# Three lists of steps laid anew in a kernel that overlaps graph convolution, attention and experts

## The chip, the cores and the metric

The kernel runs on one core of one Trainium2 chip. The metric is the device time of one execution in microseconds (us), as the median of three runs. The engines are PE (TensorE, with its weight loads PEld), DVE (VectorE), ACT (ScalarE), POOL (GpSimd) and SP (SyncE, which here only issues DMAs).

## What is computed

The input is `x`, 16 images of 256 channels on 16 x 16 positions. Cut to what matters:

```python
def reference(x, ...):
    x = x + conv(group_norm(x))          # "L0": two attentions over time and channels, three
                                         # Chebyshev products, a 1x3 convolution, relu, a layer norm
    t = tokens(x)                        # 16 x 256 tokens of 256 features
    t = t + linear_attention(ln(t))      # "L1": causal, 16 heads, phi = elu + 1, then Wo and bias
    t = t + ffn(ln(t))                   # 16 routed experts of 64 (4 chosen per token) + shared 512
    return from_tokens(t)
```

All products are to float32 accuracy. Products with the QKV and expert weights are made of three fp32r products of high and low parts (`mm3`, lines 518 to 520); the others are plain float32 matmuls.

## The kernel before

The 16 images go through as 8 pairs (0 to 7). Of each pair there are five chains of steps, and a step is a few instructions on one or several engines:

- conv (room for one pair at a time from pair 2 on): `gn` (group norm statistics), `xg` (normalise, DVE L918), `xT0 xT1` (transposes, PE L1282, copied by ACT L735), `M prod Epre Eexp Erep lr p2` (the two small attentions), `sp0 sp1` (PE L1345, softmax: DVE maxima L980, ACT exponentials L769), `rv0 rv1` (reciprocals), `st0 st1` (transposes and three products with Chebyshev matrices, DVE L996), `Y0 Y1` (PE L1244), `o0 o1` (PE L1362, 24 matmul records each), `tc0 tc1`.
- tail: `xb` (POOL), `z1` (means), `z2` (variances and a Newton root, DVE L1008 to L1025), `z3` (scale and add: DVE L1031 and L1034 for one image, POOL L689 and L692 for the other).
- attn: `tok0 tok1 nrm xl0 xl1` (layer norm and transposes), `k0 .. q1`, `kt kv`, `dent` (denominators), `rd` (SP writes the denominators to HBM and reads them back spread over partitions), then for four groups `S00 V00 S01 V01 S10 V10 S11 V11` (scores, PE L1230; causal mask, DVE L1084; weighted sums in the PSUM bank `num`, PE L1448 and L1259), `at0 at1` (DVE L1090: `num` times the spread denominators), `wo0 wo1` (DVE L1094 adds).
- route: `tk0 tk1` (transposes; statistics DVE L863, root POOL L698), `nrm2` (ACT L797), `xn0 xn1` (PE L1393), `lg` (logits), `r1 r2 r3 r4 cb` (choice of experts).
- ffn, 12 steps `j`: `gu` (24 products for gate and up), `h` (silu on ACT, product on DVE), `w` (weight of the routed expert on DVE, high part on ACT, low part on POOL), `dn` (12 products into `d_ps`).

Beside them there are steps that occur once: `hot0` to `hot23` (two PE matmul records each on constants, L1267, whose result nobody reads), and `high0` to `high13` (ACT L716) with `low0` to `low13` (DVE L858), which split 14 pieces of the weights, each loaded by one DMA, into high and low parts. `gu0` of pair 0 needs 7 pieces split.

One list, PROGRAM, is the order of all steps, and each engine goes through it and issues its own part of every step. It is put together from three tables: OPENING (pairs 0 to 2, written `pair:step`), BODY (repeated for five turns, with `+n` for the next n ffn steps of the pair that is in its experts), CLOSING (pairs 6 and 7). Every engine is in order, so a step that waits holds up everything behind it on its engine. The PSUM bank of a step is its place in the list modulo 4 (`ring`), and a step waits until the bank's user four fills before has been read.

Two waits matter below. SP issues all loads of the start, among them pieces 0 to 3. Before it issues pieces 4 to 13, and therefore before everything it takes from PROGRAM, it waits for the end of `z3` of pair 1, whose room the pieces overwrite:

```python
                if i == EARLY_PIECES:
                    sp.wait_ge(tail_dve.of(1), tail_dve.at(1, "n30"))
                    sp.wait_ge(tail_pool.of(1), tail_pool.at(1, "n31"))
                sp.dma_start(PIECES[i][3], PIECES[i][0]).then_inc(piece_loaded[i], 16)
```

And `at0` waits both for the sums and for the spread denominators, while `V10` on PE waits for `at0`, which frees `num`:

```python
                    dve.wait_ge(pv_done.of(p), pv_done.at(p, f"V{b}1"))
                    dve.wait_ge(dens_spread, 16 * 2 * (p + 1))
```

Of the kernel before, what the change touches and what calls it, by code (L numbers as in the profile page):

```python
# [118 lines left out]
OPENING = """
    0:gn 1:gn 0:xg 0:xT0 1:xg 0:M 0:xT1 0:Y0 2:gn 0:prod 1:xT0 0:high0 0:Epre 1:M 1:xT1 0:Eexp 1:Y0 1:prod 0:hot0 2:xg  # L120
    0:hot1 0:Erep 0:hot2 1:Epre 1:Eexp 0:lr 2:xT0 0:p2 1:Erep 2:M 0:high1 1:lr 0:sp0 0:rv0 0:xb 1:p2 0:sp1 0:st0
    0:hot3 2:xT1 0:hot4 0:hot5 0:rv1 0:Y1 1:sp0 0:st1 0:o0 0:low0 0:o1 0:low1 1:rv0 0:tc0 0:tc1 1:sp1 2:Y0 0:z1 0:hot6
    1:st0 2:prod 1:rv1 0:hot7 1:Y1 0:z2 0:hot8 1:st1 1:o0 2:Epre 2:Eexp 0:z3 0:high2 1:o1 0:tok0 0:tok1 0:hot9 1:tc0
    1:tc1 0:nrm 0:hot10 0:hot11 1:xb 1:z1 0:hot12 0:low2 0:hot13 2:Erep 0:xl0 0:xl1 0:hot14 1:z2 0:k0 2:lr 0:k1 1:z3
    0:v1 0:q0 0:high3 0:v0 0:kt 0:q1 0:high4 2:p2 0:hot15 0:hot16 0:hot17 0:dent 0:high5 0:high6 0:kv 0:hot18 0:rd
    0:low3 0:S00 0:hot19 2:sp0 0:V00 0:low4 0:S01 2:rv0 2:sp1 0:low5 0:at0 0:V01 0:S10 2:st0 2:rv1 0:high7 0:hot20
    0:V10 0:low6 0:S11 0:hot21 0:hot22 0:V11 2:Y1 0:hot23 0:at1 0:wo0 0:low7 0:wo1 0:high8 0:low8 0:tk0 0:tk1 0:nrm2
    0:high9 2:st1 2:o0 0:xn0 0:xn1 1:tok0 0:high10 1:tok1 1:nrm 2:o1 0:high11 0:low9 0:low10 0:lg 0:low11 1:xl0 1:xl1
    +1 0:r1 +1 1:k0 0:r2 1:k1 0:r3 +3 0:high12 0:high13 1:v1 0:silu 0:r4 1:q0 0:cb 2:xb +1 1:v0 1:kt +1 0:low12 1:q1
    +1 0:low13 +3 1:dent 2:tc0 2:tc1 +1 1:kv +2 1:rd +1 1:S00 +3 0:exp +1 1:V00 1:S01 +2 1:at0 +1 1:V01 +1 1:S10 +3  # L130
    2:z1 +1 1:V10 +1 1:S11 +2 1:V11 2:z2 1:at1 +4 2:z3 1:wo0 +2 1:wo1 +4 1:tk0 1:tk1 +4 1:nrm2 +2 1:xn0 1:xn1 +1 1:exp
"""
# [13 lines left out]


# [1436 lines left out]
```

## Time and profile before

| what | us |
|---|---|
| median of 3 runs | 931.02 (929.78 to 932.94) |
| span of the profiled execution | 958.6 |
| PE busy in it | 920.9 |
| DVE / ACT / POOL busy | 630.1 / 434.7 / 229.5 |
| start of `gu0` of pair 0 on PE | 176.9 |

The profile shows one execution, for which the page gives its span alone; that is 27.6 us longer than the median of the runs. The span has three parts: an opening up to the first `gu0`, in which PE is partly idle; from there to about 936 us PE is busy in almost every slice; and a short end. The clock column of the page is the share of TensorE's clock that was granted: 0.85 for most of the time up to about 416 us, and 0.95 after that.

### The profile page before, as it was taken

The page shows a single profiled execution, that of the slowest core. Times are in us where ns is not written, and L with a number is a line of the kernel's source. Part 1 is how long each engine was busy: PE and PEld are TensorE (multiplying, and loading weights), DVE is VectorE, ACT ScalarE, POOL GpSimd, SP SyncE. Part 2 cuts the span into 40 slices and gives each one's busy share as a digit, 9 for nine tenths or more (in the row PEclk, how much of TensorE's full clock was granted, in tenths as well). Part 3 has the DMA queues.
Part 4 walks back from the last instruction along what each step waited for, and adds up shares of the span by engine and source line. Part 5 has one row for each costly group of instructions (what it writes and reads, how often), then busy time and mean ns, then how long its engine had stood idle before and what let it go on. Part 6 is the DMA issues. An engine that isn't in the chain of part 4 may idle for free.

```text
span 958.6 us, 19446 instructions
## 1 busy us (share of the span) xinstructions
PE 920.9 (96%) x7824; PEld 802.4 (84%) x7824; DVE 630.1 (66%) x1637; ACT 434.7 (45%) x837; POOL 229.5 (24%) x198
## 2 busy tenths in 40 slices
PE   4998988999999999999999999999999999999997
PEld 2576756888898889889898889988898888988997
DVE  5546785777597447965588638975588738774532
ACT  2344443652365524645267334655257434832432
POOL 2113300113221124212241124212241124212222
PEclk9887788888888888899999999999999999999998
DMA  6000050031001110021101110021101200021021
GB/s 228 1 1 1 1 189 1 1 92 36 23 13 59 35 34 23 13 71 34 34 24 35 59 34 23 13 71 34 34 24 34 61 13 23 19 76 35 20 83 34
DMA packets 37961, 39.21 MB, mean 41 GB/s; under 512 B 5232, under 2 KB 34416, under 8 KB 37872
## 3 DMA queue, kind: packets, MB, share of 16 engines
q1 hardware_dynamic: 37872, 37.96, 12.6%
q8 instruction: 63, 1.03, 0.5%
q14 instruction: 26, 0.21, 0.1%
HBM read 32.97 MB, written 4.98 MB: 40 GB/s over the span
## 4 chain that ended last, share of the span: by engine, by line
PE 85%; DVE 10%; ACT 2%; issue 2%; DMA 1%; SPq 0%; POOLq 0%; POOL 0%; DVEq 0%; ACTq 0%
PE ring L1362 10%; PE g_ps L518 5%; PE d_ps L518 4%; PE d_ps L520 4%; PE d_ps L519 4%; PE g_ps L520 4%; PE u_ps L520 4%; PE g_ps L519 4%; PE u_ps L519 4%; PE u_ps L518 4%; PE ring L1230 4%; PE ring L1345 3%; PE num L1259 3%; PE ring L518 3%; PE ring L520 3%; PE ring L519 3%
## 5 line engine op out<-in xcount | busy, mean ns | idle before, releaser
L704 POOL TENSOR_TENSOR hl<-hb,hh 128x512 fp32r<-128x512 f32 x96 | 125.9, 1311 | 424.1 <-ACT hh L835 424.0
L835 ACT ACTIVATE hh<-hb 128x512 fp32r<-128x512 f32 x96 | 60.7, 632 | 137.0 <-DVE hb L1202 116.1
L518 PE MATMUL d_ps<-hh,down_h 128*128 128x256 f32 x384 | 116.6, 304 | 3.0 <-POOL hl L704 2.2
L518 PE MATMUL g_ps<-normed_h,gate_h 128*128 128x256 f32 x352 | 110.0, 312 | 0.2
L519 PE MATMUL d_ps<-hl,down_h 128*128 128x256 f32 x384 | 109.2, 284 | 0.0
L520 PE MATMUL d_ps<-hh,down_l 128*128 128x256 f32 x384 | 109.0, 284 | 0.0
L520 PE MATMUL g_ps<-normed_h,gate_l 128*128 128x256 f32 x352 | 100.2, 285 | 0.0
L520 PE MATMUL u_ps<-normed_h,up_l 128*128 128x256 f32 x352 | 100.1, 284 | 0.0
L519 PE MATMUL u_ps<-normed_l,up_h 128*128 128x256 f32 x352 | 100.0, 284 | 0.0
L519 PE MATMUL g_ps<-normed_l,gate_h 128*128 128x256 f32 x352 | 100.0, 284 | 0.0
L518 PE MATMUL u_ps<-normed_h,up_h 128*128 128x256 f32 x352 | 99.9, 284 | 0.0
L1197 DVE TENSOR_TENSOR hb<-sl,u_ps 128x512 f32<-128x512 f32 x88 | 60.1, 683 | 52.6 <-PE u_ps L520 38.0
L1084 DVE TENSOR_TENSOR shared<-ring,constants 128x512 f32<-128x512 f32 x128 | 79.4, 683 | 18.3 <-PE ring L1230 18.3
L518 PEld LDWEIGHTS d_ps<-hh,down_h 128*128 128x128 f32 x384 | 73.7, 192 | 8.3 <-issue 4.6
L832 ACT ACTIVATE sl<-g_ps 128x512 f32<-128x512 f32 x88 | 52.5, 597 | 59.2 <-PE g_ps L520 58.7
L518 PEld LDWEIGHTS g_ps<-normed_h,gate_h 128*128 128x128 f32 x352 | 67.4, 191 | 11.9 <-issue 6.5
L519 PEld LDWEIGHTS d_ps<-hl,down_h 128*128 128x128 f32 x384 | 73.7, 192 | 1.0 <-issue 0.3
L520 PEld LDWEIGHTS d_ps<-hh,down_l 128*128 128x128 f32 x384 | 73.8, 192 | 0.0
L519 PEld LDWEIGHTS g_ps<-normed_l,gate_h 128*128 128x128 f32 x352 | 67.8, 192 | 3.6 <-issue 3.2
L519 PEld LDWEIGHTS u_ps<-normed_l,up_h 128*128 128x128 f32 x352 | 67.6, 192 | 0.0
L518 PEld LDWEIGHTS u_ps<-normed_h,up_h 128*128 128x128 f32 x352 | 67.6, 192 | 0.0
L520 PEld LDWEIGHTS u_ps<-normed_h,up_l 128*128 128x128 f32 x352 | 67.6, 192 | 0.0
(402 smaller groups left out, 2166.2 us busy)
## 6 DMA issues: line engine op xcount, KB each, us to landing
weights_over_hidden<-weights_by_expert SPq DMA_DIRECT2D x128, 128.0 KB, 3.0
shared<-denominators_by_head SPq DMA_DIRECT2D x16, 256.0 KB
out_x<-kept SPq DMA_DIRECT2D x16, 256.0 KB, 2.2
...
raw_weights<-in_gateT SPq DMA_DIRECT2D x4, 384.0 KB, 6.7
raw_weights<-in_upT SPq DMA_DIRECT2D x4, 384.0 KB, 5.5
raw_weights<-in_down SPq DMA_DIRECT2D x4, 384.0 KB, 8.5
...
```

Of the source, the lines that this page charges most:

```text
L518: eng.matmul(ps, wh, xh, start=start, stop=False, **how)
L519: eng.matmul(ps, wh, xl, start=False, stop=False, **how)
L520: return eng.matmul(ps, wl, xh, start=False, stop=stop, **how)
L704: pool.tensor_tensor(hl[:, j % 2, :], hb, hh[:, j % 2, :].bitcast(F32), ALU.subtract).then_inc(*ffn_pool.mark(p, f"lo{j}"))
L832: act.activation(sl, gate_up(p, j)[0][:, :], ACT.Silu).then_inc(*ffn_act.mark(p, f"si{j}"))
L835: act.activation(hh[:, j % 2, :], hb, ACT.Copy).then_inc(*ffn_act.mark(p, f"hi{j}"))
L1084: dve.tensor_tensor(p_s[:, j, :].rearrange("p (h l) -> p h l", h=4), tile(p, n)[:, :].rearrange("p (h l) -> p h l", h=4), const_at("causal ...
L1197: dve.tensor_tensor(hb, sl, gate_up(p, j)[1][:, :], ALU.mult).then_inc(*ffn_dve.mark(p, f"h{j}"))
L1230: last = pe.matmul(tile(p, n)[:, 2 * c * P:(2 * c + 2) * P], k_f[rows, c, cols], q_eo[rows, :, c, cols], start=True, stop=True, tile_posit ...
L1259: last = pe.matmul(num[rows, c * L + lc * P:c * L + lc * P + P], v_s[:, b, lc, 4 * c + j, 16 * odd:16 * odd + 32], p_s[:, j, (2 * c + odd) ...
L1345: last = pe.matmul(t[:, kc * N:(kc + 1) * N], vs_s[:, jc, kc * P:(kc + 1) * P], g.th[:, b, jc, :], start=(jc == 0), stop=(jc == 1))
L1362: last = pe.matmul(t[:, c * N:(c + 1) * N], g.y_s[b][:, m, c, k], g.a_s[:, k, m, :], start=(k == 0 and m == 0 and c == 0), stop=(k == 2 an ...
```

## The change

The three tables are written anew. Every step occurs as often as before, within each chain the steps stand in one common order for all pairs, and the instructions, buffers, waits and constant products of a step are the same. What changes is where steps stand against those of other chains and pairs. The core of the diff (the rest of the tables is of the same kind):

```diff
 OPENING = """
-    0:gn 1:gn 0:xg 0:xT0 1:xg 0:M 0:xT1 0:Y0 2:gn 0:prod 1:xT0 0:high0 0:Epre 1:M 1:xT1 0:Eexp 1:Y0 1:prod 0:hot0 2:xg
...
+    0:high0 0:gn 0:xg 0:high1 0:xT0 1:gn 0:M 0:xT1 0:hot0 0:Y0 1:xg 2:gn 0:prod 0:hot1 0:low0 1:xT0 2:xg 1:M
+    1:xT1 2:xT0 0:Epre 0:hot2 1:Y0 0:hot3 0:Eexp 2:M 1:prod 2:xT1 0:hot4 0:Erep 1:Epre 2:Y0 0:hot5 0:high2
...
 BODY = """
-    +1 tok0 tok1 lg +1 gn +1 nrm +3 xg r1 +1 xl0 xl1 +1 xT0 r2 +2 M k0 xT1 k1 +2 Y0 r3 silu +1 prod r4 v1 Epre cb Eexp
...
+    +1 tok0 tok1 lg +1 gn +1 nrm +1 r1 +1 xg +3 xl0 xl1 xT0 M r2 +1 k0 xT1 k1 +1 r3 +1 silu +1 Y0 +1 prod r4
...
```

In CLOSING, `6:lg` now stands between `7:tok0` and `7:tok1`, and `7:exp` before the last experts of pair 6 in place of the middle of those of pair 7.

What this does to the engines' own orders is shown at three places.

**Place 1, the opening, DVE.** Before, from `z3` of pair 1 (its row sums lie in `hb`, its squares in `raw_weights`) over `q0`, `q1`, `p2` of pair 2, `dent` and `kv`:

```order
L1031 TENSOR_TENSOR kept<-kept,hb 128x2x256
L1034 TENSOR_TENSOR kept<-kept,raw_weights 128x2x256
L1050 TENSOR_SCALAR shared<-shared 128x512
L1052 SCALAR_TENSOR_TENSOR shared<-ring,shared 128x512
L1063 TENSOR_TENSOR shared<-shared 128x512
L1050 TENSOR_SCALAR shared<-shared 128x512
L1052 SCALAR_TENSOR_TENSOR shared<-ring,shared 128x512
L1063 TENSOR_TENSOR shared<-shared 128x512
L970 TENSOR_TENSOR first<-ring,bs_s 128x512 x2
L1070 TENSOR_SCALAR one_over_denominator<-ring 128x128
L1072 RECIPROCAL one_over_denominator<-one_over_denominator 128x128
L1065 TENSOR_TENSOR shared<-ring,constants 128x512
```

Now (line numbers are 2 higher), from `q1` over the maxima of `sp0` of pair 2, `dent`, `kv` and `z3` of pair 1 to the masks of `S00`, the reciprocal and maxima of pair 2, one split and the masks of `S01`:

```order
L1052 TENSOR_SCALAR shared<-shared 128x512
L1054 SCALAR_TENSOR_TENSOR shared<-ring,shared 128x512
L1065 TENSOR_TENSOR shared<-shared 128x512
L982 TENSOR_REDUCE conv_small<-ring 128x2
L1072 TENSOR_SCALAR one_over_denominator<-ring 128x128
L1074 RECIPROCAL one_over_denominator<-one_over_denominator 128x128
L1067 TENSOR_TENSOR shared<-ring,constants 128x512
L1033 TENSOR_TENSOR kept<-kept,hb 128x2x256
L1036 TENSOR_TENSOR kept<-kept,raw_weights 128x2x256
L1086 TENSOR_TENSOR shared<-ring,constants 128x512 x4
L986 RECIPROCAL conv_small<-conv_small 128x2
L982 TENSOR_REDUCE conv_small<-ring 128x2
```

`z3` of pair 1 has moved from ahead of `q0` to directly ahead of the masks of `S00`.

**Place 2, every turn of the body, DVE.** Before, from `wo1` over `h9`, `w9`, the statistics of `tk0 tk1`, `h10`, `w10` and the shift of `nrm2` to `z3` of the next pair:

```order
L1094 SCALAR_TENSOR_TENSOR kept<-ring,small_parameters,kept 128x512
L1197 TENSOR_TENSOR hb<-sl,u_ps 128x512
L1202 TENSOR_TENSOR hb<-hb,weights_over_hidden 128x512
L863 BN_STATS tst<-ring 128x6 x4
L514 MEMSET carrier 1x1
L870 BN_AGGR tmv<-tst 128x2 x4
L872 TENSOR_SCALAR tve<-tmv 128x4
L1197 TENSOR_TENSOR hb<-sl,u_ps 128x512
L1202 TENSOR_TENSOR hb<-hb,weights_over_hidden 128x512
L876 SCALAR_TENSOR_TENSOR shift<-tmv,trs 128x4
L1031 TENSOR_TENSOR kept<-kept,row_sums 128x2x256
L1034 TENSOR_TENSOR kept<-kept,filters 128x2x256
```

Now:

```order
L1096 SCALAR_TENSOR_TENSOR kept<-ring,small_parameters,kept 128x512
L1199 TENSOR_TENSOR hb<-sl,u_ps 128x512
L1204 TENSOR_TENSOR hb<-hb,weights_over_hidden 128x512
L1033 TENSOR_TENSOR kept<-kept,row_sums 128x2x256
L1036 TENSOR_TENSOR kept<-kept,filters 128x2x256
L865 BN_STATS tst<-ring 128x6 x4
L516 MEMSET carrier 1x1
L872 BN_AGGR tmv<-tst 128x2 x4
L874 TENSOR_SCALAR tve<-tmv 128x4
L1199 TENSOR_TENSOR hb<-sl,u_ps 128x512
L1204 TENSOR_TENSOR hb<-hb,weights_over_hidden 128x512
L878 SCALAR_TENSOR_TENSOR shift<-tmv,trs 128x4
```

The two instructions of `z3` have moved from behind the shift to ahead of the statistics; POOL's two of the same step move with them.

**Place 3, the start, ACT.** Before, the end of `Y0` of pair 0, then the first split (`high0`, L716):

```order
L747 ACTIVATE kept<-ring 128x2x2x32
L744 ACTIVATE shared<-ring 128x12x32
L747 ACTIVATE kept<-ring 128x2x2x32
L752 ACTIVATE shared<-shared 16x32
L735 ACTIVATE raw_weights<-ring 128x512
L716 ACTIVATE wqkv_h<-raw_weights 128x768
L756 ACTIVATE shared<-shared 16x32
L735 ACTIVATE raw_weights<-ring 128x512
```

Now, from the first instruction that computes:

```order
L713 ACTIVATE router<-small_parameters 128x2x16
L718 ACTIVATE wqkv_h<-raw_weights 128x768 x2
L737 ACTIVATE shared<-ring 128x512 x2
L746 ACTIVATE shared<-ring 128x12x32
L749 ACTIVATE kept<-ring 128x2x2x32
L746 ACTIVATE shared<-ring 128x12x32
```

The first two splits have moved ahead of the first transposed copy of pair 0.

## Rows read from the trace of the kernel before

**Rows 1.** The page: busy time, share of the span and instructions of each engine.

```profile
PE 920.9 (96%) x7824; PEld 802.4 (84%) x7824; DVE 630.1 (66%) x1637; ACT 434.7 (45%) x837; POOL 229.5 (24%) x198
```

**Rows 2.** Windows: length, busy time of PE, PEld, DVE, ACT, POOL, granted clock, DMA.

```profile
0.00:13.00 13.00, 1.22 (x5) 1.06 (x5) 6.23 (x36) 1.51 (x2) 4.67 (x16) 1.00 0.88 277
13.00:177.00 164.00, 147.36 (x1001) 107.85 (x1002) 103.65 (x248) 68.13 (x168) 27.22 (x23) 0.84 0.12 40
...
263.40:379.20 115.80, 115.80 (x975) 101.52 (x973) 77.10 (x203) 53.30 (x104) 28.27 (x23) 0.85 0.11 34
...
598.30:706.60 108.30, 108.15 (x974) 96.12 (x973) 76.19 (x203) 53.20 (x104) 28.32 (x23) 0.95 0.12 36
```

**Rows 3.** Windows again, the same columns, three stretches of the opening.

```profile
13.00:38.50 25.50, 22.07 (x152) 14.06 (x152) 15.04 (x59) 8.96 (x28) 4.98 (x4) 1.00 0.20 73
...
76.00:79.00 3.00, 3.00 (x36) 2.44 (x36) 1.03 (x2) 1.31 (x5) 0.00 (x0) 0.51 0.00 0
...
107.00:113.00 6.00, 5.33 (x18) 3.22 (x18) 5.46 (x18) 1.73 (x4) 2.32 (x2) 0.50 0.00 0
```

**Rows 4.** Timeline of PE, opening: start, length, operation, idle before and its releaser.

```profile
16.13 1.12 PE L1282 MATMUL ring<-constants,shared 128*128 128x128 f32 x4
18.09 2.09 PE L1244 MATMUL ring<-theta_s,shared 32*128 32x128 f32 x32 [0.84 <-ACT shared L735]
...
23.10 0.42 PE L1311 MATMUL ring<-shared,ve_h 16*64 16x32 f32 x2
...
50.89 0.66 PE L1282 MATMUL ring<-constants,first 128*128 128x128 f32 x4
...
57.44 12.21 PE L1362 MATMUL ring<-shared 128*128 128x256 f32 x48
```

**Rows 5.** The start: timeline of ACT, of SP, and the page's DMA row.

```profile
23.70 0.83 ACT L716 ACTIVATE wqkv_h<-raw_weights 128x768 fp32r<-128x768 f32 x1
...
9.24 0.94 SPq L586 DMA_DIRECT2D raw_weights<-in_wqkvT  x2
...
raw_weights<-in_wqkvT SPq DMA_DIRECT2D x2, 384.0 KB, 6.9
```

**Rows 6.** Timeline of DVE, from `z3` of pair 1 to `at0` of pair 0.

```profile
119.73 0.67 DVE L1031 TENSOR_TENSOR kept<-kept,hb 128x512 f32<-128x512 f32 x1
120.42 0.69 DVE L1034 TENSOR_TENSOR kept<-kept,raw_weights 128x512 f32<-128x512 f32 x1
...
129.19 2.48 DVE L1084 TENSOR_TENSOR shared<-ring,constants 128x512 f32<-128x512 f32 x4 [0.58 <-PE ring L1230]
...
140.67 0.69 DVE L1090 TENSOR_TENSOR shared<-num,shared 128x512 f32<-128x512 f32 x1 [0.65 <-DMA shared<-denominators_by_head]
```

**Rows 7.** Timeline of SP's queue, and its own waits (us in total, times, longest).

```profile
121.14 0.33 SPq L586 DMA_DIRECT2D raw_weights<-in_gateT  x1
...
127.41 0.70 SPq L609 DMA_DIRECT2D denominators_by_head<-one_over_denominator  x1
135.11 1.26 SPq L612 DMA_DIRECT2D shared<-denominators_by_head  x2
...
SPq L612 <- DMA denominators_by_head<-one_over_denominator: 22.6, 8, 7.0
```

**Rows 8.** Timeline of PE: the last part of `V01`, and `V10`, of pair 0.

```profile
138.88 1.19 PE L1259 MATMUL num<-shared,v_s 128*32 128x128 f32 x32
...
144.30 1.16 PE L1259 MATMUL num<-shared,v_s 128*32 128x128 f32 x32 [0.68 <-DVE shared L1084]
```

**Rows 9.** Timelines of DVE, POOL, ACT and PE in one turn of the body.

```profile
587.84 1.42 DVE L863 BATCH_NORM_STATS2 tst<-ring 128x6 f32<-128x256 f32 x4
...
590.06 1.02 POOL L698 TENSOR_TENSOR trs<-tve,minus_half 128x4 f32<-128x4 f32 x1
...
593.04 1.91 ACT L797 ACTIVATE shared<-ring,shift,trs 128x256 f32<-128x256 f32 x4
...
595.10 1.08 PE L1393 MATMUL ring<-constants,shared 128*128 128x128 f32 x8 [0.26 <-ACT shared L797]
```

More of the change, by code:

```diff
@@ L119 @@
 OPENING = """
-    0:gn 1:gn 0:xg 0:xT0 1:xg 0:M 0:xT1 0:Y0 2:gn 0:prod 1:xT0 0:high0 0:Epre 1:M 1:xT1 0:Eexp 1:Y0 1:prod 0:hot0 2:xg
[L121 to L129, printed above, removed]
@@ L130 @@
-    +1 0:low13 +3 1:dent 2:tc0 2:tc1 +1 1:kv +2 1:rd +1 1:S00 +3 0:exp +1 1:V00 1:S01 +2 1:at0 +1 1:V01 +1 1:S10 +3
-    2:z1 +1 1:V10 +1 1:S11 +2 1:V11 2:z2 1:at1 +4 2:z3 1:wo0 +2 1:wo1 +4 1:tk0 1:tk1 +4 1:nrm2 +2 1:xn0 1:xn1 +1 1:exp
+    0:high0 0:gn 0:xg 0:high1 0:xT0 1:gn 0:M 0:xT1 0:hot0 0:Y0 1:xg 2:gn 0:prod 0:hot1 0:low0 1:xT0 2:xg 1:M
+    1:xT1 2:xT0 0:Epre 0:hot2 1:Y0 0:hot3 0:Eexp 2:M 1:prod 2:xT1 0:hot4 0:Erep 1:Epre 2:Y0 0:hot5 0:high2
+    0:hot6 1:Eexp 0:lr 1:Erep 1:lr 0:p2 1:p2 0:sp0 0:rv0 1:sp0 1:rv0 2:prod 0:sp1 0:st0 1:sp1 2:Epre 0:rv1
@@ new lines @@
+    0:hot7 0:hot8 0:hot9 0:Y1 2:Eexp 0:hot10 0:st1 0:low1 0:high3 1:st0 0:o0 0:o1 0:xb 0:tc0 0:tc1 1:rv1 1:Y1
+    0:z1 2:Erep 0:z2 0:z3 1:st1 1:o0 0:tok0 0:tok1 0:nrm 0:low2 1:o1 0:xl0 0:xl1 1:tc0 1:tc1 0:k0 0:k1 0:v1
+    1:xb 0:q0 2:lr 1:z1 0:v0 0:hot11 0:kt 2:p2 1:z2 0:q1 2:sp0 0:dent 0:hot12 0:kv 0:rd 0:hot13 0:hot14 1:z3
+    0:S00 2:rv0 2:sp1 0:high4 0:low3 0:V00 0:S01 0:hot15 0:hot16 2:st0 0:at0 0:V01 0:high5 0:high6 0:hot17
+    0:S10 0:high7 0:hot18 0:V10 2:rv1 0:low4 0:high8 0:S11 0:low5 0:hot19 0:hot20 0:hot21 0:hot22 0:V11 2:Y1
@@ new lines @@
+    0:at1 0:high9 0:high10 0:low6 0:low7 0:low8 0:hot23 0:wo0 0:wo1 0:tk0 0:tk1 0:nrm2 2:st1 2:o0 0:xn0 0:xn1
+    1:tok0 0:high11 0:high12 1:tok1 0:low9 0:high13 1:nrm 2:o1 0:low10 +1 0:low11 +1 0:lg 0:r1 1:xl0 +1 1:xl1
+    0:r2 0:r3 +3 1:k0 1:k1 +1 0:silu 1:v1 0:r4 +2 2:xb 0:cb 1:q0 1:v0 1:kt 1:q1 2:tc0 2:tc1 +2 1:dent 0:low12
+    +1 1:kv +3 1:rd 1:S00 0:exp +1 0:low13 1:V00 +3 1:S01 1:at0 +1 1:V01 +3 1:S10 +3 1:V10 +3 2:z1 +3 1:S11
+    +2 1:V11 1:at1 +2 2:z2 1:wo0 1:wo1 2:z3 +1 1:tk0 +3 1:tk1 +5 1:nrm2 +1 1:xn0 1:xn1 1:exp +1
@@ L132 @@
 """
 BODY = """
-    +1 tok0 tok1 lg +1 gn +1 nrm +3 xg r1 +1 xl0 xl1 +1 xT0 r2 +2 M k0 xT1 k1 +2 Y0 r3 silu +1 prod r4 v1 Epre cb Eexp
-    q0 v0 kt q1 Erep +2 lr dent kv +3 rd S00 +2 V00 S01 +1 p2 at0 +1 V01 S10 +2 sp0 +1 rv0 +1 sp1 st0 +1 rv1 Y1 V10
-    st1 +1 o0 +3 S11 +2 V11 o1 at1 xb +2 tc0 tc1 z1 wo0 +4 z2 wo1 +4 tk0 tk1 +4 nrm2 +1 z3 +1 xn0 xn1 +1 exp
+    +1 tok0 tok1 lg +1 gn +1 nrm +1 r1 +1 xg +3 xl0 xl1 xT0 M r2 +1 k0 xT1 k1 +1 r3 +1 silu +1 Y0 +1 prod r4
+    v1 cb Epre Eexp q0 v0 kt q1 +2 Erep dent kv +1 rd lr +2 S00 +2 p2 +1 V00 +1 S01 at0 +2 V01 S10 +2 sp0 rv0
@@ L138 @@
+    sp1 +1 st0 +1 V10 +2 S11 +1 rv1 +1 Y1 xb V11 +1 at1 st1 o0 +1 o1 tc0 tc1 +1 z1 wo0 +4 z2 +1 wo1 +3 z3 tk0
+    tk1 +4 nrm2 +2 xn0 xn1 +1 exp
 """
 CLOSING = """
-    +1 7:tok0 7:tok1 +2 7:nrm 6:lg +1 7:xl0 +2 7:xl1 +1 6:r1 6:r2 6:r3 +1 7:k0 6:silu 6:r4 6:cb 7:k1 +2 7:v1 7:q0 +2
-    7:v0 7:kt 7:q1 +3 7:dent 7:kv 7:rd +3 7:S00 +2 7:V00 7:S01 +2 7:at0 +2 7:V01 7:S10 +4 7:V10 7:S11 +4 7:V11 +1
-    7:at1 +1 7:wo0 +1 7:wo1 +4 7:tk0 7:tk1 +3 7:nrm2 +2 7:xn0 7:xn1 +3 7:lg +1 7:r1 +3 7:r2 7:r3 +2 7:silu +1 7:r4
@@ L144 @@
-    7:cb +27 7:exp +22
+    +1 7:tok0 6:lg 7:tok1 +2 7:nrm +1 6:r1 +3 6:r2 +1 6:r3 7:xl0 6:silu 7:xl1 +1 6:r4 +2 6:cb +1 7:k0 7:k1
+    7:v1 7:q0 7:v0 +1 7:kt +1 7:q1 +1 7:dent 7:kv +2 7:rd +1 7:S00 +3 7:V00 +1 7:S01 +2 7:at0 7:V01 +2 7:S10
+    +1 7:V10 +1 7:S11 +4 7:V11 +3 7:at1 7:wo0 7:wo1 +2 7:tk0 7:tk1 +2 7:nrm2 +3 7:xn0 7:xn1 +3 7:lg +2 7:r1
+    +1 7:exp +3 7:r2 7:r3 +1 7:silu +1 7:r4 7:cb +50
 """
```

## Prediction

> **What bounds the kernel now.** I read the page first: PE is busy for 920.9 us, 96% of the span [rows 1], so what an order of steps can change is PE's 37.7 us of idleness, its clock, and new waits. The windows say where these lie. Up to 13 us PE did 1.2 us of work; from 13 to 177 us, when the experts of pair 0 begin, it was busy for 147.4 of 164 us, so 16.6 us idle; a body turn is full, 115.8 of 115.8 us at a granted clock of 0.85 and 108.15 of 108.3 us at 0.95 [rows 2]. A turn has hardly anything to give, and everything to lose from a new wait. The opening has 16.6 us of waits and a slow clock besides: four transposes took 1.12 us at 16 us and 0.66 us at 51 us [rows 4], which puts the first stretch at 1.2 GHz (the window shows 1.00 there only because the profile holds no clock record before 38 us), and 76 to 79 and 107 to 113 us were granted 0.5 again [rows 3].
>
> **How the profile stands to the runs.** The profiled span is 958.6 us, the median 931.02. Part of that is the clock: a turn at 0.85 takes 7.5 us more than one at 0.95 [rows 2]. The terms below are waits for DVE and DMA, which do not shorten with TensorE's clock; I work them out against the 958.6 us and add them unscaled to 931.0.
>
> **Term 1, the spread denominators of pair 0: +9 us.** This is what I rest on. Before, DVE ended `z3` of pair 1 at 121.11 (120.42 + 0.69) [rows 6]. SP had been waiting for that: it issued the ten remaining pieces from 121.14, the write of the denominators at 127.41, and their spreading reads only at 135.11, because the write landed late [rows 7]. The longest of the eight waits for that write was 7.0 us and all eight were 22.6 us, so the others took 15.6 / 7 = 2.2 us each [rows 7]: this one stood behind ten pieces of 384 KB each. `at0` started at 140.67, after 0.65 us of waiting for the spread data [rows 6]. From the end of that `z3` to `at0` is thus a chain of 140.67 - 121.11 = 19.6 us, all of it SP and DMA, and nothing in it is changed.
>
> What lies beside it is. Before, the masks of `S00` began at 129.19 [rows 6] and `V01`, the other thing that `at0` needs, ended at 138.88 + 1.19 = 140.07 [rows 8], 10.9 us later. The two chains arrived together, because `z3` came 8.1 us ahead of the masks. Now `z3` of pair 1 stands directly ahead of the masks of `S00` on DVE (place 1), behind `q1` and `kv` of pair 0, so both chains start at one point: the denominators need 19.6 us, the sums about 10. (Of the 10.9 us, two splits of 0.95 us leave the stretch on DVE, and 1.9 us of Chebyshev products of pair 2 come in ahead of `at0`.) `at0` is late by 19.6 - 10.5 = 9 us. Whatever the opening did up to there, this difference stays. Queued behind `at0` on DVE are the masks of `S10`, a split and the masks of `S11`; on PE, `V10` waits for `at0`, and everything behind it in the list, up to the first `gu0`, waits on PE. What is ahead of `V10` (`V01`, `S10`, two `hot`) covers no more than before: it is already inside the 10.9 us or follows it by 4 us, as `V10` did (144.30 [rows 8]). Bounds: 7 us if `S00` is itself held by `qo1` or the second image's maxima, 10.5 if the sums need no more than 9.
>
> **The DMA rule beside it.** The Trainium skill (DMA: Bandwidth & Descriptors, Queues, rings and completion order) says that completion is not first-in first-out per issuing engine: a later, smaller DMA can be complete while an earlier one is not. By that the 64 KB write might take the 2.2 us of the other turns rather than the 7.0 us of the row, and term 1 would be about 4 us instead of 9. The row is of this very situation and decides.
>
> **Term 2, the clock after that wait: +1 us.** PE would stand still for some 9 us. In the trace its clock was at 0.50 from 107 to 113 us, where it had waited more than once in the microseconds ahead [rows 3]. One such stretch costs half of its 5.3 us of PE work, 2.7 us, and some of the 18 us of transposes, scores and `hot` behind `V10` wait for DVE anyway. Bounds 0 and 3; I take 1. The Trainium skill (TensorE: Matmul & The Clock Gate, HAM oscillation) says that an idle gap of this kind brings the clock down and that a slow stretch costs half its length; by the rule alone I would write 3.
>
> **Term 3, the rest of the opening: 0 us, between -8 and +4.** All 24 `hot` stand ahead of the first `gu0` as before, and of real work only `lg` of pair 0 and `xl0 xl1` of pair 1 (3.1 us) now come after it, so only waits and clock count. At the start DVE saves: `xg` of pair 0 no longer stands behind the statistics of pair 1, some 3.5 us. ACT takes that away (place 3): the two splits now precede the first copy. Their pieces were issued from 9.24 and need 6.9 us [rows 5], so the second is there at about 16.8 and the copy starts 0.8 us later, near 17.7; `Y0` starts near 19 instead of 18.09 [rows 4]. Then `Epre` of pair 0 (23.10 before [rows 4]) stands behind `xg` and `xT0` of pair 2; `xg` (1.7 us of DVE) waits for a root on POOL that itself follows `Y0`'s copies. I put `Epre` at about 29, and `o0` (57.44 before [rows 4]) at about 66. But by then PE has also done `Y0` and both `sp` of pairs 2 and 1, `st0` of pair 1 and five more `hot`, some 8 us: even. The upside is the clock. At 13 to 38.5 us 22.1 us of PE work ran at the lower level and 107 to 113 another 5.3 us [rows 3], and seven `hot` instead of three now stand ahead of `p2`. If these lift the clock ten microseconds earlier, PE does that work in half the time, but copies and reciprocals between the products don't shorten. Hence -8 as one end; +4 is what `Epre`, 6 us late, could leave.
>
> **Term 4, the five turns of the body: +4 us.** (a) `z3` of the next pair now stands ahead of the statistics of `tk0 tk1` on DVE (place 2). Its two instructions take 0.67 + 0.69 us (their equals in [rows 6]), and POOL's two of the same step now precede the root there. The chain statistics 587.84, root 590.06, normalising 593.04, `xn0` 595.10 already ends last: PE waited 0.26 us for it [rows 9]. Of the 1.4 us some is absorbed, since the shift waited behind `w10` before; I take +0.5 us a turn, with 0 and 1.4 as ends. (b) At the turn's start `r1` (2.1 us of DVE) has moved ahead of `out1` and `xg`, and `M` follows `xT0` at once where an expert step stood between: +0.3 us a turn. Sum 0.8 x 5 = 4 us; bounds 0 and 8. Nothing in a full turn can pay back more than the 0.15 us that PE is idle in it [rows 2].
>
> **Closing: 0 us**, +-1: `lg` of pair 6 gives `tok1` more cover, and the table change of `7:exp` now falls where ACT already has the exponential's table.
>
> **Sum.** 9 + 1 + 0 + 4 = +14, so 931 + 14 = **945 us**.
>
> **Rivals.**
> (A) The opening gains at its front, and the wait of term 1 stays: -8 + 9 + 1 + 4 = +6, 937 us. For it: `hot` steps reach further forward. Against: the copies that pace `Y0` are on ACT and don't shorten. Chance 0.2.
> (B) Faster: the clock. With the clock at its upper level from about 20 us and never back to 0.50, PE saves up to half of (22.1 + 5.3 + three short stretches of 3 us, of which one is shown) = 36 us, 18 us; less the 14 of the other terms, this gives -4, 927 us. It decides against me from 14 us recovered, that is with more than three quarters of all slow work undone. [...] Against: term 1 makes a new idle stretch. The Trainium skill (TensorE: Matmul & The Clock Gate, Part 1) has it so, that sustained activity lifts the clock; by that rule alone B would be likelier than I make it. Chance 0.12, and with it all other ways to end faster.
> (C) The write does not queue behind the pieces, or the sums are themselves late by other waits, so that term 1 is 0 to 4 and the body keeps its 108.3 us: +0 to +4, 933 us. Chance 0.13; two fifths of it are within 0.3%.
> Forecast as summed, +9 to +20: chance 0.55.
>
> **How the numbers follow.** A measurement of this kernel tells about 0.3%, 3 us, from no change. Slower than that: the forecast, A, and three fifths of C, 0.83; the same 0.05; faster 0.12. The range runs from 930, which leaves out B's better half and a little more, to 952 (9 + 3 + 2 + 7); the forecast's own range is 940 to 951.
>
> **What would show it.** In the profile after: the `at0` of pair 0 some 19 to 20 us behind the end of `z3` of pair 1, with about 9 us of waiting for the spread DMA on DVE; PE idle for 8 to 10 us ahead of `V10`, and the granted clock at 0.50 around it; `gu0` of pair 0 some 7 to 11 us later than 176.9; turns of the body 0.5 to 1 us longer at equal granted clock, with the wait ahead of `xn0` near 0.8 us. I would be wrong if `S00` began well behind `z3`, if the clock was up from 20 us on, or if a turn lost several us at a place that I took to be covered.

## The result, and the profile after

| what | before | after |
|---|---|---|
| median, us | 931.63 (929.78 to 932.94, 4 runs) | 971.86 (971.12 to 974.49, 4 runs) |
| ratio | 1 | 1.0455, interval 1.0421 to 1.049 |
| span of the profiled execution | 958.6; 929.3 in the second profile (below) | 969.3 |
| PE busy in it | 920.9 | 900.5 |

The change costs 40.2 us. I had forecast slower, by 14. The page of the changed kernel, the row that answers to [rows 1]:

```profile
PE 900.5 (93%) x7824; PEld 792.4 (82%) x7824; DVE 651.6 (67%) x1637; ACT 427.7 (44%) x831; POOL 232.3 (24%) x198
```

Windows of the same kernel, for [rows 2] and [rows 3]: the opening, the stretch around `V10` of pair 0, a body turn from `lg` to `lg`, and the microseconds on both sides of one `xn0` of the body.

```profile
13.00:177.00 164.00, 136.61 (x982) 104.38 (x983) 104.83 (x246) 68.41 (x167) 27.85 (x23) 0.89 0.12 40
...
138.00:150.00 12.00, 2.00 (x34) 1.51 (x32) 4.01 (x7) 1.64 (x3) 0.00 (x0) 0.64 0.20 70
...
599.50:711.70 112.20, 108.17 (x976) 96.21 (x974) 79.62 (x203) 53.29 (x104) 28.61 (x23) 1.00 0.11 35
...
476.00:482.70 6.70, 4.41 (x36) 4.04 (x34) 3.64 (x8) 2.62 (x6) 4.59 (x4) 1.00 0.01 4
482.70:486.10 3.40, 3.31 (x16) 3.34 (x17) 2.01 (x4) 2.35 (x4) 0.00 (x0) 0.50 0.02 5
```

A turn of the body is now 112.2 us long, and PE is idle in 4.0 of them; in five turns that is the large part of the loss. The waits of PE, summed over the execution (us, times, longest), show where:

```profile
PE ring L1395 <- ACT shared L799: 12.3, 6, 2.4
PE num L1261 <- DVE shared L1086: 10.9, 3, 10.0
...
PE g_ps L520 <- DVE hb L1199: 4.8, 6, 1.0
```

The first row is the wait ahead of `xn0`, the second the one ahead of `V10` in the opening, the third the one ahead of `gu9`.

### The profile page after: what moved, and what is told of

It reads as the page before. It is cut to its first block, busy times and chain, and to the rows that moved or that the text cites. A ratio compares the mean times of both kernels' runs of the same rounds, so it can differ in the third digit from the quotient of the medians.

```text
span 969.3 us, 19440 instructions
## 1 busy us (share of the span) xinstructions
PE 900.5 (93%) x7824; PEld 792.4 (82%) x7824; DVE 651.6 (67%) x1637; ACT 427.7 (44%) x831; POOL 232.3 (24%) x198
## 3 DMA queue, kind: packets, MB, share of 16 engines
q1 hardware_dynamic: 37872, 37.96, 12.6%
## 4 chain that ended last, share of the span: by engine, by line
PE 71%; DVE 13%; issue 6%; POOL 3%; ACT 3%; DMA 2%; SPq 1%; POOLq 0%; DVEq 0%
PE ring L1364 8%; PE d_ps L520 4%; PE g_ps L520 4%; PE ring L1232 4%; PE d_ps L522 4%; PE d_ps L521 4%; PE num L1261 3%; PE g_ps L522 3%; PE u_ps L522 3%; PE g_ps L521 3%; PE u_ps L521 3%; PE u_ps L520 3%; PE ring L520 3%; PE ring L1347 3%; PE ring L522 3%
## 5 line engine op out<-in xcount | busy, mean ns | idle before, releaser
L520 PE MATMUL g_ps<-normed_h,gate_h 128*128 128x256 f32 x352 | 108.0, 307 | 4.9 <-DVE hb L1199 4.8
L522 PE MATMUL d_ps<-hh,down_l 128*128 128x256 f32 x384 | 108.3, 282 | 0.0
L522 PEld LDWEIGHTS g_ps<-normed_h,gate_l 128*128 128x128 f32 x352 | 66.3, 188 | 0.0
```

Source lines behind the costliest of these rows:

```text
L520: eng.matmul(ps, wh, xh, start=start, stop=False, **how)
L522: return eng.matmul(ps, wl, xh, start=False, stop=stop, **how)
```

## The experiments

**A second profile of the kernel before, and the halves of the change.** Four kernels: before unchanged, and before with one of the three changed tables.

> The kernel before, unchanged, profiled a second time, because its first profiled span (958.6 us at a granted clock of 0.90) was 27 us above its own median. Theory (the first profile was taken at a lowered clock, and the runs are not): span near 930 us, granted clock 0.97 or more outside the opening, a body turn of about 105 us (108.5 us at 0.95 and 115.8 us at 0.85, carried on to 1.00) and PE waits in a turn no longer hidden. Rival (the profile itself costs the 27 us): span again near 958 us.

> Only OPENING is the new one; BODY and CLOSING are those of before. My prediction's terms 1 to 3 are all in it. Theory P (as predicted, wait of at0 in the opening): +8 to +12 us over before, with 10 us of PE idleness ahead of V10 of pair 0. Theory Q (the wait is partly paid back by the earlier front of the opening, since gu0 of pair 0 started at 176.0 in the changed kernel and 176.9 in the first profile of before): 0 to +6 us.

> Only BODY is the new one. Theory Q (the body is where the size was missed: a turn went from about 105 us at full clock to 112.2 us): +30 to +37 us over before, the turns at 112 us with PE waits ahead of gu9, tk0 and xn0 (1.0, 0.8 and 2.5 us). Theory P (as predicted): +4 us, at most +8, turns of 106 us, and the missing 25 us are elsewhere.

> Only CLOSING is the new one. Both theories: within 2 us of before. If it is +5 us or more, the missing time is partly here, and the sum of the three lists must come to +40 us.

| kernel | median, us | ratio to before, interval | loss at 930.2 |
|---|---|---|---|
| before_again | 931.15 (one run) | | |
| opening_alone | 943.51 | 1.0148 (1.0109 to 1.0187) | 13.3 |
| body_alone | 957.17 | 1.0276 (1.0219 to 1.0333) | 27.0 |
| closing_alone | 930.21 | 1.0009 (0.9988 to 1.0030) | 0 |

The parts add up to 40.3 us. The whole change cost 40.2 us by the medians and 42 us by the ratio, so within the noise nothing is lost or gained by putting them together. Against what was expected, opening_alone lies 1.3 us above its range and body_alone 3 us below its own. The second profile of before has a granted clock of 1.00 throughout the body; the turn that answers to those of [rows 2] is this window:

```profile
463.60:571.30 107.70, 107.08 (x976) 95.52 (x974) 76.15 (x203) 53.36 (x104) 28.33 (x23) 1.00 0.13 36
```

So at full clock a turn before takes 107.7 us with 0.6 us of PE idle (not the 105 us that I had carried on from the lower clocks), and the changed turn is to be set against this one, not against the 115.8 and 108.3 us of the first profile: +4.5 us a turn.

**The opening: the write behind the pieces.** The changed opening, with only SP's order edited: first the write and the spreading reads of the denominators of pair 0, then the ten late pieces.

```diff
-            for i in range(len(PIECES)):
-                if i == EARLY_PIECES:
...
                 if name == "rd":
                     spread_denominators(p)
+                    if p == 0:
+                        late_pieces()
```

> The changed OPENING alone (943.5 us), in which SP issues the write and the spreading reads of the denominators of pair 0 first and the ten late pieces after them. Theory 1, the denominators' write is late because SP holds it behind `z3` of pair 1 and because it stands behind ten pieces of 384 KB: the reciprocal ends at 122.4, the write then lands some 3 us later and the reads are issued near 126 instead of 138.5; `at0` no longer waits 9.6 us for DMA. The pieces are issued 2 us later, and the first split of them stands between the masks of `S00` and `S01`, which can cost 2 to 3 us. Sum 943.5 - 9.6 + 2.5 = 936.4 us (933 to 939). Theory 2, the write takes its 7 us wherever it stands: the reads come at about 131, `at0` near 137, and the ten pieces are late by 8 us, for which the splits wait: 940 us or above.

Measured: 933.52 us, ratio 1.0041 (1.0023 to 1.0058), 10.0 us less than opening_alone. The changed kernel first, in the timelines of SP, DVE and PE (start, length, idle before in brackets):

```profile
126.21 0.33 SPq L588 DMA_DIRECT2D raw_weights<-in_gateT  x1
...
132.82 0.66 SPq L611 DMA_DIRECT2D denominators_by_head<-one_over_denominator  x1
139.83 1.25 SPq L614 DMA_DIRECT2D shared<-denominators_by_head  x2
...
125.50 0.69 DVE L1036 TENSOR_TENSOR kept<-kept,raw_weights 128x512 f32<-128x512 f32 x1
...
145.06 0.69 DVE L1092 TENSOR_TENSOR shared<-num,shared 128x512 f32<-128x512 f32 x1 [8.69 <-DMA shared<-denominators_by_head]
...
148.29 1.94 PE L1261 MATMUL num<-shared,v_s 128*32 128x128 f32 x32 [10.00 <-DVE shared L1086]
```

And opening_reads_first, the same engines:

```profile
123.96 0.66 SPq L613 DMA_DIRECT2D denominators_by_head<-one_over_denominator  x1
126.47 1.26 SPq L616 DMA_DIRECT2D shared<-denominators_by_head  x2
127.85 0.39 SPq L590 DMA_DIRECT2D raw_weights<-in_gateT  x1
...
136.26 0.68 DVE L1096 TENSOR_TENSOR shared<-num,shared 128x512 f32<-128x512 f32 x1
...
140.32 1.08 PE L1265 MATMUL num<-shared,v_s 128*32 128x128 f32 x32 [2.06 <-DVE shared L1090]
```

The reader is to see three things. The write alone has its reads issued 2.51 us behind it, where behind ten pieces it took 7.01. In all, the reads go out 13.4 us earlier: 4.5 us of this are the write's shorter way, and 8.9 us are SP's order, since the write no longer waits for `z3` of pair 1 and for the issue of ten pieces. `at0` starts at 136.26 with no wait, 8.8 us earlier: the sums were ready by then, as the prediction had it. And `V10` takes 1.08 instead of 1.94 us: after the 10 us of idleness it had run at the lower clock level. Theory 1 holds, and the pieces' later issue cost nothing that can be seen: DVE does not wait for one of them ahead of its splits.

**The body, `z3`.** The changed body with `z3` put back behind the statistics; with `wo1` put back too; and, in a third kernel, with only POOL's two instructions of `z3` issued behind the root.

```diff
-z2 +1 wo1 +3 z3 tk0 tk1 +4 nrm2 +2 xn0 xn1
+z2 +1 wo1 +3 tk0 tk1 +4 nrm2 +1 z3 +1 xn0 xn1
```

> The changed BODY alone (957.2 us), with `z3` put back behind the statistics of `tk0 tk1` (the turn ends `z2 +1 wo1 +3 tk0 tk1 +4 nrm2 +1 z3 +1 xn0 xn1`). Theory 1, `z3` delays the root: in the changed turns PE waits 2.4 us for the normalised tokens ahead of `xn0`, before only 0.3, and the chain to it is longer by both instructions of `z3` on DVE (1.4 us), by POOL's two of the same step ahead of the root and by a shift that takes 1.24 instead of 0.16 us. With `z3` behind, that wait is again about 0.4 us, each turn is 2.1 us shorter and the time is 957.2 - 5 x 2.1 = 946.7 us (944 to 950). Theory 2, the chain is late from its start, because `wo1` and the `kept` sums now stand one expert step later: the wait ahead of `xn0` stays above 1.5 us and the time at 954 or above.

> As body_z3_back, and `wo1` too is back ahead of `gu9` (`z2 wo1 +4` in place of `z2 +1 wo1 +3`); from `z1` on the turn is that of before. Theory 1: in the changed turns `gu9` waits 0.76 us on PE for `h8` on DVE, because nothing stands between `gu8` and it; with `wo1` in between the wait goes, and the time falls by another 5 x 0.8 = 4 us, to about 942.5 us (940 to 946). What is left over the 930.2 of before, about 12 us, is then the front half of the turn (`r1` ahead of `xg`, `M` directly behind `xT0`, `Y0`, `p2`), where the waits I can see sum to only some 0.6 us a turn, 3 us in all. Theory 2: the waits in the turn are not independent, and when the late half is restored the front half absorbs what it lost: 933 to 936 us. Theory 3, `wo1`'s place costs nothing: the time is that of body_z3_back within 1 us.

> The changed BODY alone (957.2 us), in which only POOL does its two instructions of `z3` later, behind the root of `tk1`; DVE keeps its two where the change put them, ahead of the statistics. Theory 1a, POOL is what costs: the root started 1.3 us after its variances were there because POOL was still at `z3`, and the shift took 1.24 instead of 0.16 us beside POOL; with the root ahead the first part goes, 1.3 us a turn, and the time is about 950.7 us (948 to 953). Theory 1b, DVE's 1.4 us is what costs: the statistics start as late as before, and nothing changes, 956 to 958 us. Theory 1c: the pair of POOL only moves onto the shift and slows DVE's small instructions there as much as it delayed the root: 954 to 957 us with the wait ahead of `xn0` near 2 us still.

| kernel | median, us | ratio to before, interval |
|---|---|---|
| body_z3_back | 940.52 | 1.0111 (1.0088 to 1.0134) |
| body_z3_wo1_back | 940.60 | 1.0104 (1.0078 to 1.0130) |
| body_z3_pool_later | 944.17 | 1.0158 (1.0137 to 1.0179) |

`z3` alone is worth 16.6 us by the medians (15.3 by the ratios), more than the 10.5 I had expected, and POOL's half of it 13.0 (11.0 by the ratios) where I had expected 6.5. In the changed kernel (timelines of DVE, POOL, ACT and PE, one turn):

```profile
587.98 1.41 DVE L865 BATCH_NORM_STATS2 tst<-ring 128x6 f32<-128x256 f32 x4
...
593.05 1.24 DVE L878 SCALAR_TENSOR_TENSOR shift<-tmv,trs 128x4 f32<-128x4 f32 x1 [0.91 <-POOL trs L700]
...
589.17 1.05 POOL L691 TENSOR_TENSOR kept<-kept,row_sums 128x512 f32<-128x512 f32 x1
590.30 1.29 POOL L694 TENSOR_TENSOR kept<-kept,filters 128x512 f32<-128x512 f32 x1
591.54 1.47 POOL L700 TENSOR_TENSOR trs<-tve,minus_half 128x4 f32<-128x4 f32 x1
592.99 1.28 POOL L706 TENSOR_TENSOR hl<-hb,hh 128x512 fp32r<-128x512 f32 x1
...
594.32 1.93 ACT L799 ACTIVATE shared<-ring,shift,trs 128x256 f32<-128x256 f32 x4 [1.51 <-DVE shift L878]
...
596.39 1.06 PE L1395 MATMUL ring<-constants,shared 128*128 128x128 f32 x8 [2.39 <-ACT shared L799]
```

The same chain in the second profile of before, for [rows 9]:

```profile
560.87 1.42 DVE L863 BATCH_NORM_STATS2 tst<-ring 128x6 f32<-128x256 f32 x4
...
563.10 1.02 POOL L698 TENSOR_TENSOR trs<-tve,minus_half 128x4 f32<-128x4 f32 x1
...
565.47 0.16 DVE L876 SCALAR_TENSOR_TENSOR shift<-tmv,trs 128x4 f32<-128x4 f32 x1
...
566.12 1.92 ACT L797 ACTIVATE shared<-ring,shift,trs 128x256 f32<-128x256 f32 x4
...
568.18 1.06 PE L1393 MATMUL ring<-constants,shared 128*128 128x128 f32 x8 [0.28 <-ACT shared L797]
```

This is the one turn of five in which `xn0` waits at all. The waits of PE in the first profile of before, and the same row in the second, are:

```profile
PE ring L1393 <- ACT shared L797: 0.3, 1, 0.3
```

The row in [rows 9] was thus that of one turn; in the other four the chain was covered. In the turn shown it was 7.31 us from the statistics to `xn0` and is 8.41, and the statistics themselves start behind 1.3 us of `z3` on DVE. The root starts 3.56 us after the statistics instead of 2.23, because POOL is at `z3`, and takes 1.47 instead of 1.02 us; and the shift, an instruction on 128 x 4 numbers, takes 1.24 instead of 0.16 us, because POOL begins `w10` in the same moment, having been held up. In body_z3_pool_later the root starts as soon as its input is there, but the shift is then beside POOL's `z3`, and still takes 1.02 us:

```profile
572.42 1.02 POOL L701 TENSOR_TENSOR trs<-tve,minus_half 128x4 f32<-128x4 f32 x1 [0.88 <-DVE tve L877]
573.41 1.27 POOL L692 TENSOR_TENSOR kept<-kept,row_sums 128x512 f32<-128x512 f32 x1
...
573.68 1.02 DVE L881 SCALAR_TENSOR_TENSOR shift<-tmv,trs 128x4 f32<-128x4 f32 x1
...
576.82 1.06 PE L1398 MATMUL ring<-constants,shared 128*128 128x128 f32 x8 [0.71 <-ACT shared L802]
```

From the start of `gu11` to the start of `xn0` a turn of the changed body takes 5.50 us, in body_z3_pool_later 3.71, and in the second profile of before 2.90 in four turns and 3.27 in the one shown; 2.5 us in five turns make 12.6 of the 16.6 us. Most of the rest is the clock: the last window above shows 3.4 us at 0.50 right behind the 2.3 us of idleness ahead of an `xn0`, half of which is lost, and such a stretch stands in two of the five turns of the changed body and in none of body_z3_back. That is 1.7 us for each stretch, 3.4 in all, and with the 12.6 it makes 16.0, between the 15.3 and the 16.6 measured.

`wo1` is a miss: the wait ahead of `gu9` went (it was 3.8 us in five turns), and the one ahead of `tk0` grew by 5.2 us. Waits of PE in body_z3_wo1_back, to be set against 3.1 us for the same row in body_z3_back:

```profile
PE ring L1387 <- DVE kept L1095: 8.3, 6, 1.5
```

DVE, which adds `wo1`, was late either way; theory 3 holds as long as DVE is late. Whether the place of `wo1` would cost something with DVE in time, no run shows. What makes DVE late is the next test.

**The body, `w7`.** One step moved back in body_z3_wo1_back, and the same step moved forward in the kernel before.

```diff
-o0 +1 o1 tc0 tc1 +1 z1
+o0 +2 o1 tc0 tc1 z1
```

> body_z3_wo1_back (940.6 us, turns of 109.4 us against 107.5 before) with one more place restored: `w7` ahead of `o1` instead of directly ahead of `z1` (`+2 o1 tc0 tc1 z1` in place of `+1 o1 tc0 tc1 +1 z1`). Theory 1, two engines get in each other's way: in the changed turns POOL's 1.29 us for the low part of `w7` falls on the two scalings of `z1` on DVE, which then take 2.40 instead of 1.28 us; the second `wo1` sum on DVE is 1.1 us later, and PE waits 1.66 instead of 0.52 us ahead of `tk0`. With `w7` done earlier the two scalings take 1.28 us again and the wait is back at 0.5: 940.6 - 5 x 1.1 = 935.1 us (933.5 to 937). Theory 2, `tk0` is late because `o0`, `o1` and `tc` stand later in the turn, whatever POOL does: the wait stays above 1.4 us and the time at 939 to 942. The Trainium skill (SBUF - State Buffer, Who interferes with whom) says that an instruction of VectorE with two inputs in SBUF and one of GpSimd that reads SBUF exclude each other; by that it is theory 1.

> The kernel before with one edit: `w7` directly ahead of `z1` in the body (`xb +1 tc0 tc1 +1 z1` in place of `xb +2 tc0 tc1 z1`). Theory 1: no instruction is added and DVE does nothing for `w7`, yet the two scalings of `z1` on DVE now meet POOL's low part of `w7` and take 2.40 instead of 1.28 us, and the wait ahead of `tk0` grows from 0.52 to about 1.6 us: 930.2 + 5.5 = 935.7 us (933.5 to 937). Theory 2: in this turn `tc` ends at another time than in the changed one, so the two do not meet, or the wait is elsewhere: 929 to 932 us.

Measured: body_w7_earlier 935.63 us, ratio 1.0061 (1.0039 to 1.0082), 4.0 to 5.0 us less than body_z3_wo1_back by ratio and by median; before_w7_late 935.47 us, ratio 1.0060 (1.0039 to 1.0082), 5.7 us more than before. Both theories 1. The wait of PE ahead of `tk0`, first in before_w7_late and then in the second profile of before:

```profile
PE ring L1386 <- DVE kept L1094: 8.2, 6, 1.5
...
PE ring L1386 <- DVE kept L1094: 2.6, 6, 0.9
```

In before_w7_late (timelines of DVE and POOL) the two scalings of `z1`, and a few microseconds earlier the masks of `S11`:

```profile
535.48 2.48 DVE L1084 TENSOR_TENSOR shared<-ring,constants 128x512 f32<-128x512 f32 x4 [0.41 <-PE ring L1230]
...
551.01 2.41 DVE L1004 SCALAR_TENSOR_TENSOR kept<-row_sums,kept 128x512 f32<-128x512 f32 x2
...
536.23 1.15 POOL L676 TENSOR_TENSOR filters<-x_s,small_parameters 128x512 f32<-128x512 f32 x1
...
550.97 1.29 POOL L704 TENSOR_TENSOR hl<-hb,hh 128x512 fp32r<-128x512 f32 x1 [4.46 <-ACT hh L835]
```

In the second profile of before, POOL is idle at this place and the scalings take half:

```profile
549.75 1.28 DVE L1004 SCALAR_TENSOR_TENSOR kept<-row_sums,kept 128x512 f32<-128x512 f32 x2
```

The scalings, with both inputs in SBUF, grow by 1.13 us beside 1.29 us of POOL; the masks, whose input is the PSUM bank `ring`, take their usual 2.48 us beside POOL's work.

**The body, `M`, `xg` and `r1`.** Three kernels: `dn0` again between `xT0` and `M`; `r1` again behind `xg`, with `M` left directly behind `xT0` (both on top of body_w7_earlier); and `r1` ahead of `xg` in the kernel before.

```diff
-xT0 M r2 +1 k0
+xT0 r2 +1 M k0
...
-nrm +1 r1 +1 xg +3 xl0
+nrm +2 xg r1 +3 xl0
```

> As body_w7_earlier, and `M` no longer follows `xT0` at once: `dn0` stands between them again (`xT0 r2 +1 M` in place of `xT0 M r2 +1`). Theory 1: `M` waits for ACT's copy of `xT0`, and PE's step from `xT0` to `M` took 1.27 instead of 0.36 us; with 1.5 us of other work between them 0.9 us a turn go, another 4.5 us: 930.6 us (929 to 932.5), and nothing of the body's 27 us is left. Theory 2: the copy is late anyway and the wait goes to `k0` or `xT1`: less than 2 us of gain, 933 us or above.

> As body_w7_earlier (935.6 us), `M` directly behind `xT0` as the change has it, but `r1` behind `xg` again (`nrm +2 xg r1 +3` in place of `nrm +1 r1 +1 xg +3`). Theory 1: the wait ahead of `M` is for `xg`, and `xg` is late because `r1` stands ahead of it on DVE (1.7 us) and because it then meets POOL's low part of `w0` and takes 2.7 instead of 1.75 us. With `r1` behind, `xg` takes 1.75 us and ends before `xT0` is reached, and the 0.9 us a turn go as they did with `dn0` in between: 931.1 us (929.5 to 932.5). Theory 2, what `M` waits for is ACT, as I expected of body_w7_M: `xg`'s place changes nothing, 935 us or above.

> The kernel before, with `r1` ahead of `out1` and `xg` in the body (`nrm +1 r1 +2 xg` in place of `nrm +3 xg r1`). Theory 1: `xg` meets POOL's low part of `w0` here too and takes 2.7 us, ending some 3 us later than before; the last transposes of `xT0` wait 0.3 us for it, `M` is covered by `dn0`: 5 x 0.3 = 1.5 us, 931.3 us (930 to 933). Theory 2: the delay of `xg` goes on into `Y0` and the products behind it: 934 us or above.

| kernel | median, us | ratio to before, interval |
|---|---|---|
| body_w7_M | 931.07 | 1.0014 (0.9998 to 1.0030) |
| body_xg_first | 930.24 | 1.0023 (1.0006 to 1.0040) |
| before_r1_ahead | 931.78 | 1.0025 (1.0005 to 1.0045) |

The number expected of body_w7_M came, its mechanism did not: `M` starts before ACT's copy of `xT0` ends (611.07 against 611.33 in the turn below), and reads `xg`. The changed kernel (DVE, POOL, PE), then body_xg_first:

```profile
608.21 2.71 DVE L920 TENSOR_SCALAR first<-x_s,conv_small 128x256 f32<-128x256 f32 x4
...
608.57 1.28 POOL L706 TENSOR_TENSOR hl<-hb,hh 128x512 fp32r<-128x512 f32 x1 [2.19 <-ACT hh L837]
...
609.79 0.90 PE L1284 MATMUL ring<-constants,first 128*128 128x128 f32 x4
611.07 1.07 PE L1296 MATMUL ring<-first,small_parameters 128*32 128x256 f32 x16 [0.37 <-DVE first L920]
```

```profile
471.98 1.76 DVE L919 TENSOR_SCALAR first<-x_s,conv_small 128x256 f32<-128x256 f32 x4
...
473.69 1.29 POOL L705 TENSOR_TENSOR hl<-hb,hh 128x512 fp32r<-128x512 f32 x1 [2.19 <-ACT hh L836]
...
474.93 0.60 PE L1283 MATMUL ring<-constants,first 128*128 128x128 f32 x4
475.46 1.07 PE L1295 MATMUL ring<-first,small_parameters 128*32 128x256 f32 x16
```

With `r1` ahead, `xg` meets POOL's part of `w0` and takes 2.71 instead of 1.76 us; `xT0` ends late, and `M` starts 1.28 us after `xT0` does instead of 0.53. Either cure takes all or most of it back: cover for `M` (4.5 us by the medians), or `xg` out of POOL's way (3.5 us by the ratios, which leave body_xg_first 2.1 us above before, 0.6 to 3.7). `r1`'s place alone, with the cover of `dn0`, costs 2.3 us (0.5 to 4.2) in before.

**All cures at once**, on the whole changed kernel:

> The changed kernel with the five edits together: the reads of the denominators ahead of the late pieces, and in the body `z3` behind the statistics, `wo1` ahead of `gu9`, `w7` ahead of `o1`, `dn0` between `xT0` and `M`. All else in the three lists is as changed. If the causes found are all and add up: 930.2 + 3.4 (the rest of the opening, as in opening_reads_first) + 0 + 0 = 933.6 us (931.5 to 935.5). If the two halves of the change disturb each other, or much of the loss lay in the order that is left: 938 us or above.

Measured: 935.76 us, ratio 1.0066 (1.0045 to 1.0087), 6.1 us over before. Some 34 of the 40 us are gone with five small edits. The result is 2 us above the sum I had expected. That sum put nothing for the body; by the ratios it would be 3.8 us for the opening and the 1.3 us that body_w7_M is above before, 5.1 us, and the 6.1 measured (4.2 to 8.1) cannot be told from it. No version beats the kernel before.

## Why the prediction was wrong

**Direction right, size wrong: 971.9 us against 945, outside the range to 952.** The step that failed is the fourth term, "the five turns of the body: +4 us"; it measured +27. What it lacked is POOL: its two instructions of `z3` ahead of the root were named and put at nothing (11 to 13 us), and that they and other instructions of POOL can hold up one of DVE has no price in it.

**The signs.** Those of term 1 came, as the next paragraph shows. `gu0` of pair 0 started at 176.0 us, not 7 to 11 us behind the 176.9 of the first profile. That was no gain: the 176.9 belongs to the lower clock, and the second profile of before has `gu0` at 165.6, so that it was 10.4 us later. The turns grew by 4.5 us and the wait ahead of `xn0` reached 2.4, where I had put 0.5 to 1 and 0.8; "if a turn lost several us" was the sign of being wrong that came true.

**Term 1 and 2, the denominators and the clock behind them: +10 predicted, 10.0 measured** (opening_alone less opening_reads_first). From the end of `z3` of pair 1 to `at0` it is 18.9 us (forecast 19.6), DVE waits 8.69, PE 10.0 ahead of `V10`, and in the window from 138 to 150 us the granted clock is 0.64 on the mean, 0.50 (the 1.2 GHz level) behind the wait. The write took 7.0 us behind the pieces, as in [rows 7], and 2.5 alone. The agreement to the microsecond is partly luck, since the two ratios leave some 4 us of room on either side. The DMA rule that I weighed against the row was the wrong half of its section: the Trainium skill (DMA: Bandwidth & Descriptors, Queues, rings and completion order) also says that the increment of the semaphore lands only after every earlier write of the same DMA engine; with that the page and the rows agree.

**Term 3, the rest of the opening: 0 predicted, +3.4 measured** (opening_reads_first over before, interval 2.1 to 5.4), near its upper bound of 4. In the profiles the first `gu0` is 2.2 us late (167.8 against 165.6), although the 3.1 us of `lg` and `xl0 xl1` now come behind it, so the loss lies ahead of it. PE at the front of the opening in the changed kernel, for [rows 4]:

```profile
15.43 1.12 PE L1284 MATMUL ring<-constants,shared 128*128 128x128 f32 x4
...
18.85 2.09 PE L1246 MATMUL ring<-theta_s,shared 32*128 32x128 f32 x32 [1.45 <-ACT shared L737]
...
28.25 0.42 PE L1313 MATMUL ring<-shared,ve_h 16*64 16x32 f32 x2
...
32.69 0.66 PE L1284 MATMUL ring<-constants,first 128*128 128x128 f32 x4
```

`Y0` started at 18.85 and `Epre` at 28.25, as put (19 and 29). The clock did rise at the front, four transposes taking 0.66 us at 32.69, but at 36.34 the 32 products of a `Y0` took 2.09 us again, and the rise did not pay for the rest: rivals A and B fall, and C with them, since the write did queue behind the pieces.

**Term 4, (a), `z3` ahead of the statistics: 0.5 us a turn predicted, with 1.4 as the upper end; 3.3 measured** (16.6 / 5). I named POOL's two instructions in one clause and put no number on them, though the root is the next link of the chain, and they alone are 13.0 of the 16.6 us (body_alone less body_z3_pool_later; 11.0 of 15.3 by the ratios). I also took the wait of [rows 9] for that of every turn, where it stood in one of five. Then I let the shift's wait behind `w10` absorb part of the delay; the shift grew by 1.1 us in its place. And behind the 2.4 us wait the clock came down in two of the five turns, which I had allowed for in the opening only.

**Term 4, (b), `r1` ahead of `xg`, `M` directly behind `xT0`: 0.3 us a turn predicted, about 0.9 measured** (4.5 / 5, body_w7_earlier less body_w7_M). The steps were named rightly; the size lacked POOL again.

**Missed altogether: `w7` directly ahead of `z1`, 1.0 us a turn** (5.0 / 5, with `wo1` back in its place; 5.7 / 5 in before). The prediction has no word on it, and the order of no single engine shows it: DVE does nothing for `w7`.

By the medians these are 16.6 + 5.0 + 4.5 = 26.1 of 27.0 us, and body_w7_M, which undoes all of them, cannot be told from before (ratio 0.9998 to 1.0030). Closing: 0 predicted, 0 measured.

**What the terms have in common.** The three unpriced costs all come from POOL, in two ways. With `w7` and `xg` an instruction of DVE takes about a microsecond longer because POOL works beside it. With `z3` the larger part is POOL's own order: when its two instructions went behind the root, the way from `gu11` to `xn0` fell from 5.50 to 3.71 us, although the shift still took 1.02 us beside POOL. That leaves 0.7 us a turn for the slow shift and for `z3` on DVE together. The first profile of before showed two instructions holding each other up, and I did not look for it: POOL's low part of `w10` took 1.80 us beside DVE's `z3`, in place of 1.28. The upper end of term 4 was a sum of DVE's own durations. The Trainium skill (SBUF — State Buffer, Who interferes with whom) has the rule: VectorE with two inputs in SBUF, or in a two-port mode such as `tensor_scalar` can take, excludes a GpSimd instruction that reads SBUF, and the second blocks until the first has finished. The traces agree: +1.13 us beside 1.29 (scalings of `z1`), +1.08 beside 1.28 (shift), +0.95 beside 1.28 (`xg`), nothing for the masks with their input in PSUM. Only the scalings' collision was made and unmade by itself; for the shift and `xg` the rows show the overlap, and the edits that remove it move other things too.

**The profile.** The first profile of before was of an execution at a granted clock of 0.85 to 0.95. There PE is the slower part of every race, so DVE's and POOL's delays find more cover: PE's waits ahead of `tk0` sum to 1.6 us there and to 2.6 at full clock, and "0.15 us idle in a turn" [rows 2] was 0.6. The wait ahead of `xn0` was 0.26 us there and 0.28 at full clock, so this did not hide the chain. Adding the terms unscaled was right for term 1.

**Open:** which parts of the opening make its remaining 3.4 us, what the place of `wo1` costs by itself, and whether the 1.3 us of body_w7_M over before are real.
